# Nineteen extra row gathers at the head of GpSimd's program in a graph layer, and sixteen semaphores for its input gathers

## The reference

```
feat  = relu(h @ W_pool + b_pool)
w     = edge_weight / max(segment_sum(edge_weight, dst), eps)[dst]
neigh = segment_max(feat[src] * w, dst)          (0 where a node has no edge)
rst   = h @ W1_self + neigh @ W1_neigh + b1
h2    = relu(rst / max(norm(rst), eps))
neigh2= segment_sum(h2[src] * w, dst) / max(deg, 1)
out   = x + relu(h2 @ W2_self + neigh2 @ W2_neigh + b2)
```

## Time and profile before

| | |
|---|---|
| time, median of 3 (lowest to highest) | 4112.68 us (4112.07 to 4112.8) |
| the profiled execution's own time | 4112.68 us |
| its span, first to last instruction | 4110.8 us |
| POOL busy, share of the span | 3076.6 us, 75% |
| DVE busy | 2820.1 us, 69% |
| PE busy | 2576.0 us, 63% |
| ACT busy | 1352.4 us, 33% |

### The profile page before, as it was taken

One profiled execution on the slowest core, in us unless ns is written; L12 is line 12 of the kernel. 1 busy time (PEld: TensorE's weight loads), 2 busy tenths in 40 slices (PEclk: granted clock), 3 DMA queues, 4 the chain that ended last, 5 costly groups with the idle time before them and its releaser, 6 DMA issues. The chain is left out here.

```text
span 4110.8 us, 30816 instructions
## 1 busy us (share of the span) xinstructions
PE 2576.0 (63%) x7403; PEld 1201.8 (29%) x7403; DVE 2820.1 (69%) x6223; ACT 1352.4 (33%) x3994; POOL 3076.6 (75%) x3262
## 2 busy tenths in 40 slices
PE   4133342222378777774667777777777777779856
PEld 4032232222123222221422222222222222224534
DVE  6477797877667776775567777767776777677424
ACT  5333443333333333332533233323332233323320
POOL 7777777777777777776767777777777777777766
PEclk8555555555599999997579899999998989989755
DMA  6233333334433333333433333333333333333335
GB/s 201 89 113 106 105 120 125 125 127 129 130 104 117 107 111 112 105 109 103 102 94 106 114 107 106 117 106 104 117 107 106 114 107 109 114 104 104 114 110 149
DMA packets 206026, 468.02 MB, mean 114 GB/s; under 512 B 57650, under 2 KB 123188, under 8 KB 181012
## 3 DMA queue, kind: packets, MB, share of 16 engines
q0 software_dynamic: 104000, 213.25, 18.5%
q1 hardware_dynamic: 101844, 252.80, 16.8%
HBM read 240.76 MB, written 225.06 MB: 113 GB/s over the span
## 5 line engine op out<-in xcount | busy, mean ns | idle before, releaser
L447 POOL DMA_INDIRECT G<-h_tab,SRC x1511 | 1425.7, 944 | 471.8 <-issue 420.0
L447 POOL DMA_INDIRECT G<-feat_tab,SRC x1451 | 1375.8, 948 | 442.2 <-issue 393.1
L769 DVE TENSOR_SCALAR CP<-pH,kc 128x512 f32<-128x512 f32 x1862 | 1388.4, 746 | 38.6 <-PE pM L925 36.5
L546 ACT ACTIVATE pT<-G,EW 128x128 f32<-128x128 f32 x1522 | 553.8, 369 | 1205.1 <-DMA G<-h_tab,SRC 615.3
L546 ACT ACTIVATE pM<-G,EW 128x128 f32<-128x128 f32 x1440 | 512.2, 367 | 1238.0 <-DMA G<-feat_tab,SRC 593.4
L925 PE MATMUL pM<-CP,A 128*128 128x512 f32 x1372 | 693.5, 654 | 229.8 <-DVE CP L769 229.8
L925 PE MATMUL pC<-CP,A 128*128 128x512 f32 x1176 | 632.7, 695 | 174.0 <-DVE CP L769 174.0
L901 PE MATMUL pH<-CP 128*128 128x98 bf16 x1563 | 144.6, 281 | 603.8 <-DVE CP L727 603.8
L715 DVE SCALAR_TENSOR_TENSOR S<-S,M,pT 128x128 f32<-128x128 f32 x782 | 267.1, 342 | 354.6 <-ACT pT L546 348.0
L712 DVE SCALAR_TENSOR_TENSOR S<-S,C,pT 128x128 f32<-128x128 f32 x782 | 269.7, 345 | 334.3 <-ACT pT L546 320.7
L925 PEld LDWEIGHTS pM<-CP,A 128*128 128x128 f32 x1372 | 235.2, 200 | 674.9 <-DVE CP L769 559.5
(11 more groups left out here) (134 smaller groups left out, 1814.9 us busy)
## 6 DMA issues: line engine op xcount, KB each, us to landing
scan<-S SPq DMA_DIRECT2D x97, 1032.0 KB, 4.1
scan<-S SPq DMA_DIRECT2D x97, 1024.0 KB, 4.0
G<-h_tab,SRC POOLq DMA_INDIRECT x1511
G<-feat_tab,SRC POOLq DMA_INDIRECT x1451
feat_tab<-F SPq DMA_DIRECT2D x24, 256.0 KB, 2.4
h_tab<-A SPq DMA_DIRECT2D x24, 256.0 KB, 2.6
U<-in_x SPq DMA_DIRECT2D x24, 256.0 KB, 3.7
out<-F SPq DMA_DIRECT2D x24, 256.0 KB, 2.6
```

Of the source, the lines that this page charges most:

```text
L447: pool.indirect_dma_start(out=dst, out_offset=None, in_=table, in_offset=bass.IndirectOffsetOnAxis(ap=idx, axis=0)).then_inc(s, 16)
L546: act.activation(scaled(t), v, ACT.Copy, scale=EW[:, t:t + 1]).then_inc(s_mul, 1)
L769: dve.tensor_scalar(OH[:, k % 4, :], pH[:, :], kc[:, j:j + 1], None, ALU.is_equal).then_inc(s_o2, 1)
```

## The change

```diff
-NX = 32
+NX = 16
+PARTS = [127, 126, 125, 124, 122, 120, 118, 112, 108, 100, 96, 80, 64, 48, 32, 16]
...
         s_xg = [sem(f"s_xg{i}") for i in range(NX)]
+        s_pt = [sem(f"s_pt{i}") for i in range(2)]
...
             pool.wait_ge(s_srcx, 16)
+            for i, n in enumerate(PARTS):
+                gather(G[0:n, i, :], x, SRC[0:n, i:i + 1], s_pt[0])
+            pool.wait_ge(s_pt[0], 16 * len(PARTS))
+            for i in range(3):
+                pool.indirect_dma_start(out=G[:, i, :], out_offset=None, in_=x, bounds_check=NP - 1, oob_is_err=False,
+                                        in_offset=bass.IndirectOffsetOnAxis(ap=SRC[:, i:i + 1], axis=0)).then_inc(s_pt[1], 16)
+            pool.wait_ge(s_pt[1], 16 * 3)
             for t, i in XAT.items():
                 if i >= NX:
                     pool.wait_ge(s_xg[i % NX], 16 * (i // NX))
```

## The result

The changed kernel takes 4151.81 us (median of 3, 4151.29 to 4151.81) against 4112.68: a ratio of 1.0095 with an interval of 1.0072 to 1.0118. That is 39.1 us more, where 34.9 were forecast. The spans say the same, 4149.9 - 4110.8 = 39.1 us.

A forecast was written before the change was run, and what follows sets the result against it. POOL, issuing one gather after another, was taken to bound the kernel. Short gathers, two waits and three bounded gathers delay the 88 by 34.9 us: 4112.68 + 34.9 = 4147.6 us, 8-in-10 range 4138 to 4162.

The forecast's parts named there:

- the forecast's own case: Short gathers at POOL's head cost anywhere between proportion to rows and full price: 4140 to 4150 us, chance 72%.
- uneven counts dear: Rival: on POOL, nine counts not multiples of 16 take twice a gather, 8.5 us more, about 4156 us; chance 13%.
- three signs of being wrong: Short gather clearly off 0.94 us; first wait ending after 32 us or before 25; shift at 38 differing from the end's.
- No slack on POOL: POOL issues gathers back to back, 4051 of 4110.8 us, so any delay before 114 us delays the whole rest.
- The sixteen short gathers: At POOL's head, each costs a full gather's 1.248 us with gap; the sixteenth starts at 21.8 us.
- Few engines: Rival: uneven counts go to few DMA engines and land late, 4148 to 4159 us; chance 10%.
- The first wait: After the sixteenth short gather, landing takes 6.6 us beside the loads, plus 0.26 us: POOL continues at 28.7.
- The bounded gathers: Three whole gathers with a bound after the first wait, 1.248 us each; twice a gather allowed from above.
- The second wait: After the third bounded gather, issued at 31.2, landing takes 6.6 us; POOL goes on at 38.0.
- Sixteen semaphores: In the 88 gathers, each waits for one issued 20 us before; costs nothing while landing stays under 20 us.
- the prelude's stretched gathers: In the edge pass, gathers up to 4.12 us during DVE's prelude move along with the delay, their price unchanged.

The follow-up runs named there:

- e2: The changed kernel with both waits moved behind the 88 gathers and the bounded gathers writing a free part of S: 4145.89 us, ratio 1.0067 to the kernel before.
- e6: The changed kernel with all nineteen added gathers and both waits moved behind the 88 gathers: 4149.07 us, ratio 1.0076 to the kernel before.
- e3: The changed kernel with the sixteen row counts reversed, 16 first and 127 last: 4159.78 us, ratio 1.0102 to the kernel before.
- e5: The changed kernel with sixteen gathers of 127 rows in place of the sixteen counts: 4195.45 us, ratio 1.0189 to the kernel before.
- f4: The changed kernel with sixteen gathers of 97 rows in place of the sixteen counts, on another chip: 5019.62 us, ratio 1.0045 to the kernel before there.
- e8: The kernel before with sixteen semaphores and one gather of 127 rows ahead of the 88, on another chip: 4986.43 us, ratio 1.0003 to the kernel before.
- e1: The kernel before with sixteen semaphores instead of 32 for the 88 gathers, on another chip: 4990.09 us, ratio 1.0008 to the kernel before there.
- e4: The changed kernel with sixteen gathers of 128 rows in place of the sixteen counts, on another chip: 5004.99 us, ratio 1.0038 to the kernel before there.

## Why the prediction was right, and where its sizes were off

The time fell 4.2 us from the forecast and inside the range, but 1.8 us above 4140 to 4150, the band of the forecast's own case. What came is that case and a part of a rival (uneven counts dear, 3.6 us instead of 8.5), and the width left for the rivals covers it.

Of the three signs of being wrong the first came true: 127 rows lasted 2.74 us and four other counts 1.21 to 1.68. The second was at its limit of 32 us: the landing came at 31.6, POOL's next gather at 32.35. The third did not come: the shift at the 88 is the shift at the end, to half a microsecond.

By the prediction's steps:

- **No slack on POOL** held: 39.55 us at the 88, 39.17 at the edge pass, 39.1 at the end. e2 and e6 show it in other amounts: 27.1 and 30.5 us of delay at the edge pass gave 28.1 and 31.3 at the end.
- **The sixteen short gathers** is the term that was mis-sized. The sixteenth starts at 25.66 for a forecast of 21.8. All sixteen last 18.85 us, where the full price gives 15.1 and 0.17 for the first: 3.6 us more. I took the row count to matter little, and for the seven counts that 16 divides it does (0.86 us for 16 rows, 0.94 for 112). The other nine cost 0.98 to 2.74 us. A line through these nine (127 at the 2.55 us of e3 and e5), against rows per engine at the largest divisor up to 16, gives 0.87 us + 13.2 ns a row, and f4 met it at a new point. So the uneven counts were dear, as one rival had it, but not for being uneven: by that division 126 rows on 14 engines cost 0.98, 122 on two 1.68.
- **Few engines**: I priced that rival by landing alone and let its sum stay. Its division of rows is what the durations follow, but they show it on POOL's instruction, which I hadn't thought of. Its packets were misread: a full gather is not 32 packets of four rows but 16 of eight rows and 16 small ones, and 127 rows are 272 packets, not 32 (e8). Its conclusion stood all the same: the 127 rows landed 10.0 us after their issue, for the 14.3 worked out, long before the sixteenth. The Trainium skill, DMA: Bandwidth & Descriptors, Why a DMA increments its semaphore by 16 and not by 1, gives the division and the rotation. The prices and packet counts fit the division, and the flat landing in e5 fits the rotation. The Trainium skill, DMA: Bandwidth & Descriptors, Anatomy of one DMA, calls descriptor generation "small, variable", with many descriptors to be had before they show. The counts that 16 divides agree (0.86 us for 16 rows, 0.94 for 128), the others do not (2.55 for 127).
- **The first wait** came close: 6.69 us from the start of the sixteenth to the next instruction for 6.86. Two errors cancelled: it landed in 5.9 us, not 6.6, and 0.7 us passed from there to the bounded gather instead of 0.26. A register write for the bound, 0.03 us, stands in that gap; the rest of it is not explained.
- **The bounded gathers** took 1.03, 1.00 and 0.99 us for the 0.94 taken, far from twice that.
- **The second wait** was 7.65 us for 6.86, since its gather landed in 7.4.
- **Sixteen semaphores** cost nothing (e1, and the pace of the 88 in the changed trace), and the prelude's stretched gathers moved along: the longest takes 4.11 us at 180.1, for 4.12 before.

The sum of the misses is 0.16 for a later start, 3.7 for the short gathers, -0.2, 0.1 and 0.8 for waits and bounded ones, and -0.4 for the stretched gather: 4.2 us.

## What to carry to other kernels

Where one engine issues at a steady pace from start to end, anything put on its path is paid in full, and a wait for a landing costs the landing time of that stretch: POOL stood idle for 5.8 and 6.7 us beside the bulk loads, for about 2 us when they were over (e6). Give gathers on GpSimd a row count that 16 divides, or at least one with a large divisor up to 16; the instruction itself took 2.7 times as long for 127 rows as for 128, and 1.04 times for 126. A busy share of 75% says nothing of slack: look at what ends the gaps, and look again on another chip: there the same program but for its sixteen semaphores waited 73 us at the same place, and even that was no slack (e4).

## What the runs showed that I had not expected

- A gather of 127 rows takes POOL 2.55 us and 272 packets, one of 128 takes 0.94 us and 32.
- After 7 gathers of 127 rows, and after 10 of 97, POOL pauses, in the first case until everything issued has landed, and the profile files that under "issue" (16.0, 6.2 and 14.9 us). The room lies between 970 and 1016 rows of such shares. What fills up isn't shown: with a new engine for each gather no single engine would hold so many rows, only the last two of the seven were still on their way when the second pause began, and the 2962 full gathers of the two edge passes show no such pause.
- On two other chips the kernel takes 21% longer and is bounded elsewhere, with POOL's instructions at the same 0.94 us. There the other engines pause for long while POOL issues gathers, though DVE's instructions are no longer. The cause is open.
